# Attention stages of a decoder kernel: 64-row score products, stationary values in four 32-column tiles, a selection product that turns the result back

## The reference

```
q, k, v = x Wq + bq, y Wk + bk, y Wv + bv        # y is x, or a context; 16 heads of 16 channels
s[h]    = q[h] k[h]^T / 4  (+ mask)              # 128 x 128 for each head
p[h]    = softmax(s[h])                          # over the last axis
o       = concat(p[h] v[h]);  r = x + o Wo + bo  # the last layer has no Wo
x       = layernorm(r)
```

## Time and profile before

| | us |
|---|---|
| median of 3 runs (lowest, highest) | 5760.74 (5760.74, 5765.56) |
| the profiled execution, its own time | 5752.95 |
| span in its trace | 5751.2 |

### The profile page before, as it was taken

The page is one execution under the profiler, slowest core; times in us unless marked ns, Lnnn a source line. Parts: engine busy times, 40 slices in busy tenths (PEclk is TensorE's granted clock), DMA queues, the critical chain, the costliest instruction groups (busy, mean ns, idle before and its releaser), DMA issues. The chain is left out here.

```text
span 5751.2 us, 124731 instructions
## 1 busy us (share of the span) xinstructions
PE 4003.0 (70%) x49763; PEld 2790.3 (49%) x49763; DVE 3546.3 (62%) x9363; ACT 1289.1 (22%) x2427; POOL 1073.6 (19%) x1120
## 2 busy tenths in 40 slices
PE   2676667666776754958777547757855777886897
PEld 1455555555555534745555324435532555554554
DVE  6989898889889641035544548872444454434445
ACT  1222222222222211312222311102333222321111
POOL 1322232223222132032222000000100122211000
PEclk7888888888888886978877755557866887887999
DMA  1011111110011002720000000000000000000000
GB/s 55 21 32 27 27 23 32 23 31 23 22 32 27 24 9 110 284 79 0 0 35 7 13 3 0 0 11 30 0 6 5 5 0 25 8 1 6 15 18 26
DMA packets 65147, 157.37 MB, mean 27 GB/s; under 512 B 7024, under 2 KB 54128, under 8 KB 60656
## 3 DMA queue, kind: packets, MB, share of 16 engines
q1 hardware_dynamic: 63088, 145.74, 8.3%
q0 software_dynamic: 1536, 4.20, 0.2%
HBM read 138.37 MB, written 11.53 MB: 26 GB/s over the span
## 5 line engine op out<-in xcount | busy, mean ns | idle before, releaser
L754 POOL TENSOR_TENSOR weights<-weights,arena 128x64 f32<-128x64 f32 x512 | 395.1, 793 | 1043.4 <-DVE arena L1272 1043.3
L144 POOL TENSOR_TENSOR arena<-arena,eps 128x4 f32<-128x4 f32 (+2 forms) x76 | 16.1, 212 | 2281.6 <-DVE arena L139 2281.6
L1322 DVE TENSOR_TENSOR arena<-arena 128x120 f32<-128x120 f32 (+27 forms) x1888 | 396.5, 250 | 4.3 <-DVE arena L1315 2.7
L1315 DVE TENSOR_TENSOR arena<-arena 128x120 f32<-128x120 f32 (+27 forms) x1888 | 388.4, 244 | 6.3 <-DVE arena L1322 2.8
L831 PE MATMUL psum<-arena 128*32 128x1 bf16 x639 | 114.2, 179 | 389.7 <-DVE arena L1284 307.8
L402 PE MATMUL psum<-arena 128*128 128x512 f32 x640 | 356.2, 690 | 16.8 <-ACT arena L482 11.2
L422 PE MATMUL psum<-ident,arena 128*128 128x128 f32 x1280 | 219.1, 327 | 210.6 <-ACT arena L493 210.6
L414 PEld LDWEIGHTS psum<-arena 128*128 128x128 f32 x2048 | 284.4, 217 | 101.0 <-issue 60.6
L300 POOL TENSOR_TENSOR arena<-arena,weights 128x1024 f32<-128x1024 f32 x128 | 242.3, 1900 | 405.3 <-PE psum L402 340.2
L831 PEld LDWEIGHTS psum<-arena 128*32 128x32 bf16 x639 | 60.3, 94 | 524.7 <-DVE arena L1284 270.9
L414 PE MATMUL psum<-arena 128*128 128x17 f32 x2048 | 276.5, 279 | 33.4 <-ACT arena L490 33.4
(11 more groups left out here) (451 smaller groups left out, 8530.3 us busy)
## 6 DMA issues: line engine op xcount, KB each, us to landing
arena<-in_experts_L_ffn SPq DMA_DIRECT2D x23, 2180.0 KB, 8.4
weights<-L_decay_rows SPq DMA_DIRECT2D x256, 160.0 KB, 3.5
arena<-in_ctxT SPq DMA_DIRECT2D x16, 512.0 KB, 3.3
arena<-in_experts_L_ffn SPq DMA_DIRECT2D x18, 384.0 KB, 3.0
weights<-in_w_L_ffn SPq DMA_DIRECT2D x1, 3072.0 KB, 10.0
L_ffn_x_sorted<-arena SPq DMA_DIRECT2D x1, 2944.0 KB, 10.1
arena<-L_ffn_x_sorted SPq DMA_DIRECT2D x23, 128.0 KB, 7.9
L_ffn_y_sorted<-arena SPq DMA_DIRECT2D x23, 128.0 KB, 8.2
```

The lines of the kernel that those rows point to most:

```text
L754: a = pool.tensor_tensor(blocks, bc(w.minus_eye, 1, 2), bc(beta[:, at, 2 * b:2 * b + 2], 2, Q), ALU.mult)
L1315: dve.tensor_tensor(part, bc(lanes[:, j + 1:, j], 2, n), bc(inv[:, j, cols], 1, below), ALU.mult).then_inc(s["links"], 1)
L1322: dve.tensor_tensor(inv[:, j + 1:, cols], inv[:, j + 1:, cols], part, ALU.add).then_inc(s["links"], 1)
```

## The change

Five things, all in `attention_stage` and the packing of its weights:

1. `km` has 4 blocks where it had 8. The mask of heads puts heads 0 to 3 in the upper 64 rows of these blocks and heads 4 to 7 in the lower 64. `scores` makes one product of 64 rows by 512 columns from each half of the rows; the two write different PSUM banks.
2. Causal stages: the mask goes into PSUM by two bfloat16 products (identity by mask) ahead of the scores, which accumulate on it. The DVE instruction L545 goes there; the scale moves into the exponential. L1_xattn keeps L545.
3. `values`: the values (with ones, filled up to 32 columns by zeros) are stationary, `pT` is streamed (128 columns); head h writes the 32 PSUM partitions of column tile h % 4. The result stands with channels in the partitions (`columns_psum`).
4. ACT copies that to `oc`, between the copy of pT and the exponential. `pick`, new, brings it back: four products a sequence with `oc` stationary and a selection matrix of 68 columns streamed.
5. `pick` is in even steps. DVE's two blocks for o and for the residual move to odd steps, one step later; a turn has 12 steps where it had 11. The banks of o, oT and y change places, and `shared_bank` adds waits to `values`, `turn_o` and `project_out`.

```diff
-    km = A(2, HH, P)
-    va = A(TILES, H, DH + 1)
+    km = A(2, HH // 2, P)
+    ident_h, causal_h = A(P, dtype=BF16), A(P, dtype=BF16)
+    VW = 32
+    va = None if recalled else A(TILES, H, VW)
+    vs = A(2, VW) if recalled else None
+    oc = A(2, 2, P)
...
-    STEPS = range(UNITS + 3)
+    STEPS = range(UNITS + 4)
+    causal, added = mask == "causal", mask == "batch"
...
-    o_psum = ps[:, O_BANK, 0:H * (DH + 1)].rearrange("p (h e) -> p h e", e=DH + 1)
-    oT_psum = ps[:, Y_BANK, 0:D].rearrange("p (c t) -> p c t", c=C)
-    y_psum = ps[:, Y_BANK, D:2 * D]
+    columns_psum = ps[:, O_BANK, 0:D].rearrange("p (c t) -> p c t", c=2)
+    o_psum = ps[:, Y_BANK, 0:H * (DH + 1)].rearrange("p (h e) -> p h e", e=DH + 1)
+    oT_psum = ps[:, O_BANK, D:2 * D].rearrange("p (c t) -> p c t", c=C)
+    y_psum = ps[:, O_BANK, D:2 * D]
...
-            pool.memset(va[:, :, :, DH:DH + 1], 1.0).then_inc(ones_set, 1)
+            pool.tensor_copy(ident_h, k.ident)
+            if causal:
+                pool.tensor_copy(causal_h, w.causal)
+            if recalled:
+                pool.memset(vs[:, :, DH + 1:], 0.0).then_inc(ones_set, 1)
+            else:
+                pool.memset(va[:, :, :, DH + 1:], 0.0)
+                pool.memset(va[:, :, :, DH:DH + 1], 1.0).then_inc(ones_set, 1)
...
-                pool.tensor_tensor(km[:, j % 2, :, :], bc(keys, 1, HH), bc(w.heads, 2, P), ALU.mult
+                pool.tensor_tensor(km[:, j % 2, :, :], bc(keys, 1, HH // 2), bc(w.heads, 2, P), ALU.mult
...
+                pool.tensor_tensor(km[:, u % 2, :, :], bc(keys, 1, HH // 2), bc(w.heads, 2, P), ALU.mult)
+                v = k.Y[:, bass.ds(g * TILES + u, 1), P:P + DH + 1].rearrange("p a e -> p (a e)")
+                pool.tensor_copy(vs[:, u % 2, 0:DH + 1], v).then_inc(keys_spread, 1)
...
+                    for b in range(2 if causal else 0):
+                        nc.tensor.matmul(out[:, b * 4:b * 4 + 4, :], ident_h, bc(causal_h, 1, HH // 2),
+                                         start=True, stop=False)
                     for b in range(2):
-                        mm = nc.tensor.matmul(out[:, b * 4:b * 4 + 4, :], qT[:, c, u * P:(u + 1) * P],
-                                              km[:, at % 2, b * 4:b * 4 + 4, :], start=True, stop=True)
+                        rows = slice(b * P // 2, (b + 1) * P // 2)
+                        mm = nc.tensor.matmul(out[:, b * 4:b * 4 + 4, :], qT[rows, c, u * P:(u + 1) * P],
+                                              km[rows, at % 2, :, :], start=not causal, stop=True)
                     mm.then_inc(scores_ready, 1)
+                def shared_bank(columns, turned, projected_out):
+                    pe.wait_ge(o_copied, g * UNITS + columns)
+                    if out_proj and turned:
+                        pe.wait_ge(oT_ready, g * TILES + turned)
+                    if out_proj and projected_out:
+                        norm.wait_added(pe, g * TILES + projected_out)
 
                 def values(j):
                     u, c = divmod(j, C)
                     pe.wait_ge(probsT_ready, g * UNITS + j + 1)
-                    if c == 0 and u >= 1:
+                    if j:
+                        shared_bank(j, max(0, (j - 1) // 2), max(0, (j - 2) // 2))
+                    for h in range(HH):
+                        rows = slice(h % 4 * VW, (h % 4 + 1) * VW)
+                        mm = nc.tensor.matmul(columns_psum[rows, h // 4, :],
+                                              vs[:, u % 2, :] if recalled else va[:, u, c * HH + h, :],
+                                              pT[:, j % 2, h, :], start=True, stop=True)
+                    mm.then_inc(o_columns, 1)
+                def pick(u):
+                    pe.wait_ge(o_copied, g * UNITS + C * u + C)
+                    if u >= 1:
                         pe.wait_ge(o_normalised, g * TILES + u)
-                    for h in range(HH):
-                        v = (k.Y[:, bass.ds(g * TILES + u, 1), P:P + DH + 1].rearrange("p a e -> p (a e)") if recalled
-                             else va[:, u, c * HH + h, :])
-                        mm = nc.tensor.matmul(o_psum[:, c * HH + h, :], pT[:, j % 2, h, :], v,
-                                              start=True, stop=True)
-                    if c == C - 1:
-                        mm.then_inc(o_ready, 1)
+                    for c in range(C):
+                        for i in range(2):
+                            at = (2 * c + i) * 4
+                            mm = nc.tensor.matmul(o_psum[:, at:at + 4, :], oc[:, c, i, :], w.pick, start=True, stop=True)
+                    mm.then_inc(o_ready, 1)
...
                 def turn_o(u):
                     pe.wait_ge(o_normalised, g * TILES + u + 1)
-                    if u >= 1:
-                        norm.wait_added(pe, g * TILES + u)
+                    shared_bank(min(UNITS, C * u + C + 1), u, u)
                     for c in range(C):
...
                 def project_out(u):
                     pe.wait_ge(oT_ready, g * TILES + u + 1)
+                    shared_bank(min(UNITS, C * u + C + 2), 0, 0)
...
+                    if j >= 2 and j % 2 == 0 and (j - 2) // 2 < TILES:
+                        pick((j - 2) // 2)
...
                         nc.scalar.copy(pT[:, (j - 1) % 2, :, :], pt_psum).then_inc(probsT_ready, 1)
+                        if j >= 3:
+                            act.wait_ge(o_ready, g * TILES + (j - 1) // 2)
+                        act.wait_ge(o_columns, g * UNITS + j)
+                        nc.scalar.copy(oc[:, (j - 1) % 2, :, :], columns_psum).then_inc(o_copied, 1)
                     if j < UNITS:
                         act.wait_ge(shifted, g * UNITS + j + 1)
                         nc.scalar.activation(pr[:, j % 2, :, :], pr[:, j % 2, :, :], ACT.Exp,
-                                             scale=1.0 if mask else DH ** -0.5).then_inc(probs_ready, 1)
+                                             scale=1.0 if added else DH ** -0.5).then_inc(probs_ready, 1)
                     if more and j == UNITS + 1:
...
-                        if mask:
-                            if mask == "batch":
-                                if j == 0:
-                                    dve.wait_ge(mask_loaded, (g + 1) * 16)
-                                m = mk[:, j // C, :]
-                            else:
-                                m = w.causal
+                        if added:
+                            if j == 0:
+                                dve.wait_ge(mask_loaded, (g + 1) * 16)
                             chain(dve.scalar_tensor_tensor(out=pr[:, j % 2, :, :], in0=s, scalar=DH ** -0.5,
-                                                           in1=bc(m, 1, HH), op0=ALU.mult, op1=ALU.add))
+                                                           in1=bc(mk[:, j // C, :], 1, HH), op0=ALU.mult, op1=ALU.add))
                             s = pr[:, j % 2, :, :]
                         chain(dve.tensor_reduce(mx[:, j % 2, :], s, AX.X, ALU.max))
                         dve.tensor_tensor(pr[:, j % 2, :, :], s, bc(mx[:, j % 2, :], 2, P), ALU.subtract).then_inc(shifted, 1)
-                    if j >= 2 and j % 2 == 0 and (j - 2) // 2 < TILES:
-                        u = (j - 2) // 2
+                    if j >= 3 and j % 2 == 1 and (j - 3) // 2 < TILES:
+                        u = (j - 3) // 2
                         dve.wait_ge(o_ready, g * TILES + u + 1)
                         chain(dve.reciprocal(ri[:, :], o_psum[:, :, DH]))
...
-                    if out_proj and j >= 4 and j % 2 == 0:
-                        u = (j - 4) // 2
+                    if out_proj and j >= 5 and j % 2 == 1:
+                        u = (j - 5) // 2
...
-    return (np.arange(P)[:, None] // DH == np.arange(HH)[None, :]).astype(np.float32)
+    return (np.arange(P)[:, None] // DH % (HH // 2) == np.arange(HH // 2)[None, :]).astype(np.float32)
+def pick_columns():
+    head, e = np.arange(P) // 32, np.arange(P) % 32
+    i, j = np.divmod(np.arange(4 * (DH + 1)), DH + 1)
+    return ((head[:, None] == i) & (e[:, None] == j)).astype(np.float32)
```

More of the change, by code:

```diff
@@ L225, in attention_stage @@
     rotated, keys_spread = sem("rotated"), sem("keys_spread")
+    o_columns, o_copied = sem("o_columns"), sem("o_copied")
     scores_ready, shifted, probs_ready = sem("scores_ready"), sem("shifted"), sem("probs_ready")
@@ L304, in recalled_keys @@
                 keys = k.Y[:, bass.ds(g * TILES + u, 1), 0:P].rearrange("p a t -> p (a t)")
-                pool.tensor_tensor(km[:, u % 2, :, :], bc(keys, 1, HH), bc(w.heads, 2, P), ALU.mult
-                                   ).then_inc(keys_spread, 1)
+                pool.tensor_tensor(km[:, u % 2, :, :], bc(keys, 1, HH // 2), bc(w.heads, 2, P), ALU.mult)
+                v = k.Y[:, bass.ds(g * TILES + u, 1), P:P + DH + 1].rearrange("p a e -> p (a e)")
+                pool.tensor_copy(vs[:, u % 2, 0:DH + 1], v).then_inc(keys_spread, 1)
```

(12 more changed lines are left out.)

## The result

The changed kernel takes 5568.2 us (median of four runs, 5560.0 to 5579.5), the kernel before 5762.4: a ratio of 0.9663, 95% interval 0.9652 to 0.9675. The direction and the chain that is left were as forecast; the size, and which part of the change carries it, were not.

The account below looks back on a forecast made before the run. DVE was taken as the chain in the masked stages, PE in L2_xattn. Gains 104 + 20 + 10 less 4 and 16 make 114: 5752.95 becomes 5639, plus 7.8 to the median 5646 us; range 5570 to 5735.

Parts of the forecast that it names:

- the chain that is left: Attention steps: DVE's waits go, ACT and PE in turn set the time from one turn_probs to the next.
- plain step: Step without pick or Wo: pT's copy, values, new copy, exponential and turn_probs in series, 4.46 us.
- `pick` alone: Step with pick but without project_out: 5.27 us, the mask's products adding 0.4.
- odd: Step with Wo: turn_o and oT's copy come first, so pT's copy starts 0.59 after turn_probs; 5.0 us.
- even: Step with pick and project_out: PE's 3.55 us hides pT's copy, then copy, exponential and turn_probs; 6.17 us.
- the 717 us: Sum of the seven-step stretches over all twenty turns, four turns of each stage, at the upper clock.
- Forecast factor 1.07: Attention stretches: mean clock stays 0.89, 22% of the time at the lower level, so 717 becomes 769 us.
- The rival of the lower clock: Seven steps: PE streams less and falls to the lower clock, 271 us more, 5917, slower; chance 0.10.
- beside these stretches: Outside the seven steps: normalisation at turns' begins 20, first mask instruction 10, filling zeros -4 us.
- 16 us charged: PE: up to three more semaphore waits a unit, 0.1 x 160 = 16 us taken as a loss.
- the 872.6: Kernel before: us in the twenty stretches from a turn's first to its eighth subtraction, seven steps each.
- The drain rule: PE: a change of tiling mode drains TensorE; three changes a unit in the chain cost 53 us, time 5686.

Follow-up runs that it names:

- copy_later: The changed kernel with ACT's copy of oc moved behind the exponential instead of before it: 5345 us, ratio 0.928.
- scores_alone: The kernel before with only the scores made by 64-row products and half the spreading: 5799 us, ratio 1.007.
- no_values: The changed kernel with values computed as before (pT stationary, 16 instructions of 17 columns), without oc and pick: 5544 us, ratio 0.963.
- more_waits: The changed kernel with three more PE waits, on semaphores long met, ahead of each unit's values: 5568 us, ratio 0.967.
- sched_mask: The kernel before with DVE's blocks for o and residual a step later and the causal mask in PSUM: 5526 us, ratio 0.959.
- no_scores: The changed kernel with scores by 128-row products and all of the spreading again: 5632 us, ratio 0.978.

## Why the prediction missed, step by step

**The chain.** Right: DVE's waits went out of the chain (most of those for o are still there, 56.6 of 77.3 us, but beside it), ACT and PE in turn are the bound, the new copy stands in it (copy_later: 224 us). Where no mask is added in PSUM: plain step 4.29 for 4.46, `pick` alone 5.07 for 5.27, odd 4.90 to 5.08 for 5.0, even 5.99 for 6.17. The last step of a turn with Wo has no next scores, and takes 5.51 where the sum had 6.17. With the mask's products a plain step takes 4.61: they need 0.59 a unit, not 0.4, and stand in the plain steps too, in which the sum had left them out. The 0.17 from pT's copy to the values is 0.05 to 0.06 in the changed kernel, because the scores in front of them end in time. Scores take 1.13, not 0.95, but beside pT's copy that costs nothing in a plain step without a mask; values (0.65) and copy (0.37) were as said. Turns at granted 1.00 take 36.8 in L1_attn and 33.8 in L3_self, against 37.7 and 34.9: the 717 us are about 697 (an estimate, scaled by these two).

**The clock.** Forecast factor 1.07, measured 737/697 = 1.06; mean 0.93, not 0.89. Worth 9 us more. The rival of the lower clock didn't come in the whole change; scores_alone and no_values show that it was near. Transposes didn't keep the clock down either: 56 of PE's 228 instructions in the L3_self turn shown above are transposes, at a granted 1.00.

**The term that failed: beside these stretches.** Forecast 20 + 10 - 4 = 26, measured 61. One turn's end in L1_attn, from the eighth `turn_probs` to the next first, goes from 41.8 to 36.5 us: the mask's instruction 1.2, as forecast; normalisation 0.85 of the up to 1.9; the first subtraction 0.7 (1.91 beside POOL's spread, 1.22 from PSUM), not seen; the last projections and residuals 1.3 and the projection of the next turn 1.2 (15.09 to 13.90), because the clock is back at its upper level earlier, not seen either. Before, with PE's windows (us, busy, granted clock) at the end:

```profile
2707.68 15.09 PE L377 MATMUL psum<-arena,weights 128*128 128x512 f32 x32
...
2724.12 5.03 DVE L154 TENSOR_SCALAR X<-arena 128x256 f32 x3 [0.15 <-DVE X L154]
...
2732.19 1.91 DVE L549 TENSOR_TENSOR arena<-arena 128x1024 f32<-128x1024 f32 x1
...
2704.00:2707.70 3.70, 2.92 (x10) 0.50 0.00 0
2707.70:2710.00 2.30, 2.30 (x4) 0.50 0.00 0
```

After:

```profile
2695.53 13.90 PE L393 MATMUL psum<-arena,weights 128*128 128x512 f32 x32
...
2710.78 4.18 DVE L154 TENSOR_SCALAR X<-arena 128x256 f32 x3 [0.15 <-DVE X L154]
...
2716.73 1.22 DVE L589 TENSOR_TENSOR arena<-psum,arena 128x1024 f32<-128x1024 f32 x1
...
2691.80:2695.50 3.70, 2.71 (x15) 0.86 0.00 0
2695.50:2700.00 4.50, 4.50 (x12) 1.00 0.00 0
```

I had ended the clock's account at the eighth step. I had also misread the 1.46 us of the earlier trace rows: it is a mean of 76 subtractions of 1.22 and 20 of 1.9 to 2.5, and those 20 have POOL's work beside them; without it, reading SBUF costs no more than reading PSUM.

**The waits.** 16 us charged; as many again cost nothing (more_waits).

**The sum.** 16 for the waits, 21 for the steps (20 x 1.07), 9 for the clock and 35 beside them make 81; 12 go off since the 872.6 between subtractions held 12 that now count as turn ends, and 11 for the late start: 58 of the 60 by which the spans miss. The other 18 of the 78 between 5646 and 5568 come from the two profiled executions: I had added 7.8 because that of before lay under its median, and that of after lies 11.3 over its own. I had no term for that in the range.

**The drain rule.** A unit has three changes of tile shape. In the plain step above the values start 0.04 us after the scores' modelled end (4021.11) and 0.06 after pT's copy (4021.09), and the scores before the transposes' modelled end; the 0.2 charged in even steps was not seen (5.99 for 6.17), and the 5686 did not come. What the Trainium skill, TensorEngine Tiling (Array Packing), Key Properties, says would show best in copy_later, where nothing else delays PE: there four groups fill 3.16 us, and their durations leave no gap between them. A drain hidden inside a group's duration no run here excludes.

**What the prediction did not say.** It counted the later blocks in one sentence and gave the products the numbers. The runs put it the other way round: the later blocks alone give all of the gain, the mask some 35 us more, scores and values together less than nothing (5526 to 5568) as long as the new copy stands before the exponential, and 181 us (5526 to 5345) once it doesn't. Apart, in the first case: the values cost 106 (sched_mask 5526 to no_scores 5632), and the scores give 64 back. Why the clock falls in some of these kernels and not in others stays open.

## What to carry to other kernels

Where an engine waits for a result that nobody needs soon, move that block behind the work that others wait for before you shorten any product; undo and do each part alone, since a change of four parts can owe its time to one. A faster path that needs a new copy can cost more than it gives, as long as the copy stands ahead of what the next unit waits for. And an engine that is busy all the time may still be at half its clock: read the granted clock of every stretch, up to the end of the turn.

## Of the hardware, not expected

- PE busy 97% of a stretch had a granted clock of 0.58 in one kernel and 0.99, at 96%, in another.
- Two 64-row products on the two row halves overlap, but not wholly: four instructions of 512 columns take 1.13 us where four of 128 rows take 1.88.
- Waits that are already met are free: 480 more of them, 5567.98 against 5568.2.
- POOL's work beside DVE stretches some of DVE's operations and not others: four normalisations take 5.00 beside two spreads of 1.9 and 3.44 beside two of 1.04, where one alone takes 0.41. In the kernel before, a subtraction with both operands in SBUF takes 1.22 alone (76 times) and 1.9 to 2.5 beside POOL (20 times). With one operand in PSUM it takes 1.22 in both cases, and so does the maximum, also where it reads SBUF (60 times alone, 36 beside POOL).
